# An attention and feed-forward kernel: four orders of loads on the SyncE queue

## The reference

```python
# x: (4, 1024, 512), ctx: (4, 2048, 512); 16 heads of width 32; all in float32
n = layernorm(x)
q, k, v = n @ W_q.T, ctx @ W_k.T, ctx @ W_v.T            # split into 16 heads
e = exp(clip(q @ k.T / sqrt(32), -50, 50))               # per head; mask keeps all rows
x = x + ((e / e.sum(-1)) @ v) @ W_o.T
n = layernorm(x)
# feed-forward: rows of n and columns of rhs scaled to whole numbers in -127..127
x = x + (round(n / s_n) @ round(rhs / s_r)) * s_n * s_r
```

## Time and profile before

| | |
|---|---|
| median of 3 runs | 1706.11 us (1705.11 to 1706.46) |
| the profiled execution's own time | 1705.6 us |
| its span | 1703.8 us |
| TensorE busy | 1671.9 us, 98% of the span |
| VectorE busy | 1489.7 us, 87% |
| ScalarE busy | 1314.5 us, 77% |
| GpSimd busy | 133.7 us, 8% |
| DMA queue of SyncE | 287.64 MB, 66.5% of 16 engines |
| on the chain that ended last | TensorE 82%, ScalarE 6%, DMA 5%, VectorE 4% |

### The profile page before, as it was taken

How to read it: one execution, slowest core, us unless ns; L and a number is a source line. 1 busy time by engine, 2 the same in 40 slices (tenths; PEclk the granted TensorE clock), 3 DMA queues, 4 the chain that set the end, 5 groups by cost and what they waited for, 6 DMA issues and landing times.

```text
span 1703.8 us, 29863 instructions
## 1 busy us (share of the span) xinstructions
PE 1671.9 (98%) x10418; PEld 1009.7 (59%) x10448; DVE 1489.7 (87%) x1705; ACT 1314.5 (77%) x1730; POOL 133.7 (8%) x75
## 2 busy tenths in 40 slices
PE   9999999999999999999999999999999999999998
PEld 8896655656565565656666566565656444444445
DVE  5657888888897989999898998989999889999997
ACT  5557788888887877877777787877878778788875
POOL 0000000000001111011110101111011000000001
PEclk9999999999999999999999999999999999999999
DMA  8687656566666566756657576566756799988971
GB/s 280 211 233 187 145 139 152 154 168 170 145 163 167 143 176 168 197 137 165 179 134 206 127 192 165 144 186 159 199 134 155 180 210 205 217 180 204 214 172 62
DMA packets 235059, 294.85 MB, mean 173 GB/s; under 512 B 28184, under 2 KB 142360, under 8 KB 234392
## 3 DMA queue, kind: packets, MB, share of 16 engines
q1 hardware_dynamic: 231688, 287.64, 66.5%
q10 hardware_dynamic: 3216, 5.24, 1.1%
HBM read 201.07 MB, written 91.48 MB: 172 GB/s over the span
## 4 chain that ended last, share of the span: by engine, by line
PE 82%; ACT 6%; DMA 5%; DVE 4%; issue 2%; SPq 1%; ACTq 0%; POOL 0%; POOLq 0%; DVEq 0%
PE wsum L999 25%; PE tile L962 24%; PE scores L984 21%; ACT probs L1247 5%; PE scores L1148 3%; PE scores L962 2%; DVE acc L1552 2%; PE tile L1148 1%; PE tile L1031 1%; DMA q_stack<-q_parts 1%; DMA row_lo<-o_parts 1%; DMA o_parts<-sums 1%; PE tile L1111 1%; DMA q_parts<-q_stack 1%; PE tile L1088 1%
## 5 line engine op out<-in xcount | busy, mean ns | idle before, releaser
L1247 ACT ACTIVATE probs<-scores 128x1024 f32<-128x1024 f32 x939 | 914.7, 1026 | 207.8 <-PE scores L984 169.3
L1552 DVE TENSOR_TENSOR acc<-acc,probs 128x2048 f32<-128x2048 f32 x439 | 1003.1, 2285 | 39.9 <-ACT probs L1247 25.3
L999 PE MATMUL wsum<-probs,v_sb 128*32 128x512 f32 x4096 | 492.4, 598 | 0.0
L984 PE MATMUL scores<-q_stack,k_stack 128*128 128x512 f32 x1536 | 444.5, 409 | 2.5 <-ACT probs L1247 1.7
L984 PEld LDWEIGHTS scores<-q_stack,k_stack 128*128 128x128 f32 x1536 | 264.9, 188 | 213.2 <-ACT probs L1247 121.3
L999 PEld LDWEIGHTS wsum<-probs,v_sb 128*32 128x32 f32 x4096 | 106.9, 109 | 243.9 <-issue 230.0
L1654 POOL TENSOR_TENSOR rstd<-var_eps,minus_half 128x1 f32<-128x1 f32 x48 | 105.9, 2207 | 1186.7 <-DVE var_eps L1446 1186.7
L1552 DVE TENSOR_TENSOR acc<-probs 128x2048 f32<-128x2048 f32 x32 | 73.4, 2293 | 56.7 <-PE tile L1031 51.2
L1148 PE MATMUL scores<-q_stack,k_stack 128*128 128x512 f32 x342 | 109.6, 421 | 8.6 <-ACT probs L1247 8.6
L962 PE MATMUL tile<-ctx_hi,wk_hi 128*128 128x256 f32 x412 | 116.4, 283 | 0.0
L962 PE MATMUL tile<-ctx_hi,wk_lo 128*128 128x256 f32 x412 | 116.0, 282 | 0.0
(11 more groups left out here) (255 smaller groups left out, 1988.4 us busy)
## 6 DMA issues: line engine op xcount, KB each, us to landing
k_stack<-k_parts SPq DMA_DIRECT2D x312, 256.0 KB, 7.8
q_stack<-q_parts SPq DMA_DIRECT2D x124, 256.0 KB, 7.2
v_sb<-v_parts SPq DMA_DIRECT2D x80, 256.0 KB, 7.5
v_parts<-v_stage SPq DMA_DIRECT2D x64, 256.0 KB, 5.0
raw<-ctxT SPq DMA_DIRECT2D x27, 512.0 KB, 5.6
k_parts<-stage_hi SPq DMA_DIRECT2D x96, 128.0 KB, 4.7
k_parts<-stage_lo SPq DMA_DIRECT2D x96, 128.0 KB, 2.5
x_in<-x SPq DMA_DIRECT2D x33, 256.0 KB, 4.2
```

Of the source, the lines that this page charges most:

```text
L984: last = nc.tensor.matmul(scores[:, h, :], k_stack[:, kt // 4, h, (kt % 4) * P:(kt % 4 + 1) * P], q_stack[:, qb, h, :], start=True, stop=True)
L999: last = nc.tensor.matmul(wsum[DH * h:DH * h + DH, :], v_sb[:, kt, DH * h:DH * h + DH], probs[:, n % RING, h, :], start=(kt == 0), stop=(k ...
L1247: nc.scalar.activation(probs[:, slot % RING, 2 * pair:2 * pair + 2, :], score_banks(seg, slot, pair), ACT.Exp, scale=1.0 / math.sqrt(DH)). ...
L1552: nc.vector.tensor_tensor(acc[:, :, :], other, probs[:, slot % RING, :, :], ALU.add).then_inc(sems["add_done"], 1)
```

## The change

Only the order of SyncE's instructions changes, with one semaphore name on TensorE.

```diff
-ROW_LOADS = {0: 0, 1: 5, 2: 5, 3: 5, 4: 1, 5: 1, 6: 7, ...}
+ROW_LOADS = {0: 0, 1: 5, 2: 4, 3: 4, 4: 1, 5: 1, 6: 7, ...}
# final_steps
                     if slot == 5 and c == 0:
-                        load_o_rows(sp, 0, slice(0, G), slice(P, QB), "rows_loaded5")
+                        load_o_rows(sp, 0, slice(0, G), slice(P, 2 * P), "rows_loaded5")
+                    if slot == 14 and c == 0:
+                        load_o_rows(sp, 0, slice(0, G), slice(2 * P, QB), "rows_loaded4")
...
-                        if step == 8:
+                        if step == (6 if i == 0 else 8):
                             load_q(sp, j_next, qb_next, (i + 1) % 2)
# iteration
-                    if seg.s == 0 and slot == 12:
+                    if seg.s == 1 and slot == 2:
+                        load_last()
+                    if seg.s == 1 and slot == 6:
                         load_weight("o", woT)
-                        load_last()
...
-                            if slot == KT + 4 * quarter + 5:
+                            if slot == KT + 4 * quarter + 5 + (quarter == 2):
                                 ct.wait_alone(sp, "scores_full", 2 * (KT + 4 * quarter + 4))
                                 load_k(sp, j + 1, quarter)
-                            if slot == KT + 4 * quarter + 6 + (quarter == 0) - (quarter == 2):
+                            if slot == KT + 4 * quarter + 6 + (quarter == 0):
                                 ct.wait_alone(sp, "step_summed", KT + 4 * quarter + 4)
                                 load_v(j + 1, quarter)
```

More of the change, by code:

```diff
@@ L161 @@
 D_BEFORE = order_of_the_bank()
-ROW_LOADS = {0: 0, 1: 5, 2: 5, 3: 5, 4: 1, 5: 1, 6: 7, 7: 7, 8: 2, 9: 2, 10: 6, 11: 6}
+ROW_LOADS = {0: 0, 1: 5, 2: 4, 3: 4, 4: 1, 5: 1, 6: 7, 7: 7, 8: 2, 9: 2, 10: 6, 11: 6}
 class Segment:
```

## The result

The kernel after takes 1754.49 us (median of 6 runs, 1751.27 to 1756.39) against 1706.28 us before (6 runs on the same chip): a ratio of 1.0278, with a 95% interval from 1.0265 to 1.029. It is slower, as forecast, but by 48 us where the forecast had 18, and it lies outside the range of 1706 to 1735. The profiled execution took 1751.27 us with a span of 1749.5, which is 45.7 us over the span of before.

The account below looks back on a forecast made before the run. The prediction took TensorE, busy 1671.9 of 1703.8 us, to bound the kernel. Its terms, -3.2 - 1.1 + 22.8 - 0.6 = +17.9 us on 1705.6, gave 1723.5, predicted as 1724, with a range from 1706 to 1735.

Parts of the forecast that it names:

- The opening, -3.2: Opening: weights issued behind the first stores remove TensorE's 1.70 us wait and 1.54 us of slow clock; -3.2 us.
- Changes of batch, -1.1: Two changes of batch: result stores ahead of keys shorten TensorE's waits for stage C's rows; -1.1 us, bounds -2.4 and +1.5.
- Nine borders, +22.8: Borders within batches: Q2's store behind keys delays ScalarE's cast and TensorE; 6 x 2.3 + 3 x 3.0 = +22.8 us.
- the second pair of heads: Nine borders: TensorE stands 0.3 us more at each, between the two pairs of heads.
- rival B: Nine borders: gaps also lower TensorE's clock, 1.54 us more at each, +13.9, giving 1738 us; chance 0.10.
- The last batch, -0.6: Last batch: the queries' wait goes, but `safe_row` lands later behind keys; net -0.6 us, bounds -1.5 and +2.5.
- 1 us of it comes out at the block's end: Last batch: VectorE's first sum starts some 3 us later, of which 1 us was counted as cost.
- The -1.5 for the queries: Last batch: TensorE's 1.48 us wait for the second block's queries goes once they move ahead of the keys.
- Rivals A: Nine borders: stores pass the keys or ScalarE's delay is hidden, so they cost nothing; 1701 us, chance 0.14.
- C: Nine borders: Q2's store lands 7 us after the first key issue, +4.2 us in all; 1705 us, chance 0.09.
- the two halves of the rule: DMA queues: descriptors are taken in ring order, holding a store behind keys; completion isn't first in, first out, letting it pass.

Follow-up runs that it names:

- experiments 1: The kernel after with the third quarter of keys and values back in slot 29 at every part; 1702.94 us, ratio 0.9976.
- experiment 8: The kernel before with: opening's edit alone, 1702.21 us; last batch's edits alone, 1703.71 us; opening's edit and quarter moved at ends of batches 0 and 1, 1701.91 us.
- experiments 2: The kernel before with only the third quarter of keys and values moved to slot 30; 1753.30 us, ratio 1.0273.
- experiments 3: The kernel after with the third quarter of keys and values moved only at the ends of batches 0 and 1; 1701.74 us, ratio 0.9974.
- experiment 4: The kernel after with the third quarter of keys and values issued, within a batch, behind the stores of Q2 and Q3; 1741.06 us, ratio 1.02.
- 5: The kernel after with Q2's and Q3's four stores issued, within a batch, from ScalarE's queue behind its exponentials of slot 31; 1722.93 us, ratio 1.0112.
- Experiment 7: The kernel after with small products ahead of slot 2's scores in batch 0's three borders: 24 products, 1750.98 us; 14 products, 1750.81 us.
- experiment 9: The kernel after with: quarter back within batches, behind `safe_row` in batch 2, 1704.29 us; `safe_row` on GpSimd's queue, 1752.99 us; that with keys mostly back, 1703.42 us.
- experiment 6: The kernel after with only the third quarter's values in slot 30, 1700.98 us; with only its keys in slot 30, 1731.14 us.
- the last of 8: The kernel before with the opening's loads moved and the quarter moved only at the ends of batches 0 and 1; 1701.91 us, ratio 0.9976.
- the first two of 8: The kernel before with the opening's edit alone, 1702.21 us; and with only the last batch's edits, 1703.71 us.
- the last run of experiment 9: Opening as in after, keys late only at ends of batches 0 and 1, values late except batch 2's end, `safe_row` on GpSimd's queue, queries ahead; 1703.42 us.

## Why the prediction was wrong in size

- **The opening, -3.2.** Measured -3.35 in the profiled execution. As a step it stood, but its 1.54 us of clock belonged to that one execution of before: two unchanged openings ran 1.70 and 2.45 us ahead of it, with PEclk 1.00. That the number came out so near is partly luck.
- **Changes of batch, -1.1.** Measured -2.7, a little past the low bound of -2.4. Both waits of the earlier trace rows are gone: the rows land 3.4 us behind TensorE's last mark of the batch (534.7 against 531.35) where they took 5.3 (522.8 against 517.43); I had forecast a gain of 1.2 us for 2.0 measured. Part of this belongs to the one execution of before as well. With the quarter left in its place, three other executions (experiments 1 and 8) stepped by -0.08, -0.43 and -1.46 us at the first change and by +0.15, -0.38 and +0.06 at the second; with it moved, they stepped by -0.6 to -2.4 and by -0.1 to -1.0 in experiments 2 to 5 and 7 to 9. And since the values alone bring as much (experiment 6), the keys ahead of the result were not the whole of what made its rows late, as my sum had it.
- **Nine borders, +22.8. This is the step that failed, by its size.** The mechanism is shown (experiments 1, 2, 4 and 6): loads issued ahead of the store, buffer, cast, exponential, scores, in the order forecast. The term measured 47.5 us, for three reasons. Q2's store landed 10.1 us after the first key issue, where I took 9.0, between the two cases of its own kind, 9.7 and 9.8, and a key load with little around it; even my high bound was 9.8. That makes the idle time 30.1 us instead of the 20.1 forecast (2.0 and 2.7 a border; the rest of the 22.8 was 0.3 a border for the second pair of heads). Then I put the lower clock aside as rival B, with a chance of 0.10, because two gaps of 1.86 and 1.48 us had been followed by full clock; but the gaps I was forecasting were longer, 2.3 and 3.0 us, and the only evidence I had against B came from shorter ones. B was not another way for it to go; it was part of the same sum. But shorter gaps are not safe either: in experiment 6 the clock fell behind 1.79 us and not behind 2.13. The Trainium skill tells in "TensorE: Matmul & The Clock Gate", "HAM oscillation — how this bites in real kernels", of a loop whose wait for a DMA, some 3 to 5 us, comes back in every round, so that every round starts with the array at the low clock. The nine gaps here, 2.44 to 4.24 us, did the same. Last, I counted 0.3 us for the second pair of heads, where ScalarE's delay costs TensorE about 0.9 us behind the gap. Experiment 7 splits what lies behind the gaps of batch 0 in halves: 1.0 us a border of clock, 0.9 of this. For the other six the split was not measured directly (experiment 6 puts the clock at 1.2 us a border); the two make 17.4 us over the nine, where the sum had 2.7.
- **The last batch, -0.6.** Measured +4.3, outside -1.5 to +2.5. `safe_row` took 4.5 us as forecast (4.7), and VectorE was 2.35 us late for my 3. What I guessed, that 1 us of it comes out at the block's end, can't be read from this one execution. Experiments 4 and 7 (with 24 products) have the same instructions in the last batch, `safe_row` in 4.5 and 4.4 us, and VectorE 2.4 and 2.2 us late, and their last batch steps by +1.45 and +1.25, within my bounds. VectorE's first sum in experiment 4, 34.8 us after its counterpart of before where TensorE's lag is 32.4:

```profile
1370.78 2.29 DVE L1560 TENSOR_TENSOR acc<-probs 128x2048 f32<-128x2048 f32 x1 [1.17 <-POOLq L1688]
```

The first block costs 1.7, 1.7 and 1.5 us in the three. The second costs 2.7 in the kernel after and nothing in the other two, so the late flag doesn't force it. The -1.5 for the queries was wrong: the 1.5 us came back as waits for VectorE (experiments 1 and 8). The rows in two pieces cost nothing by themselves: with them, the queries ahead and an early flag the last batch steps by +0.1 (experiment 8).

- **Rivals A and C** (hidden, 1701 and 1705) are excluded by the borders' rows: no landing came under 9.2 us. (By the prediction's own sum C costs 1.0 us, not 0.8, at a border of batch 0, which changes nothing.) B, 1738, named the clock and was still short, since it left the landing and the second pair as they were. Of the two halves of the rule that the prediction weighed (the Trainium skill, "DMA: Bandwidth & Descriptors", "Queues, rings and completion order"), the nine landings agree with the order of the ring, and no store here passed the loads ahead of it in its own queue.

Open: why `safe_row` took 3.7, 2.9 and 3.5 us in experiments 3 and 1 and the last of 8, where before took 1.80 and the first two of 8 took 1.95 and 1.69, with the same issues ahead of it in all six. Open too is what makes the last batch's second block cost 2.7 us in some executions and nothing in others, and whether it was a queue or the order of issue over all queues that held the stores.

## What to carry to other kernels

When a load is moved ahead of a store in a queue, price the wait of whoever writes that store's buffer next, by landings of the same kind (stores behind such loads: 9.7 and 9.8 us here, for 10.1 measured), and don't shade them towards faster ones of another kind. An idle gap on TensorE in a kernel at full clock can have three prices, not one: the gap, the slower clock behind it, and the engine that fed it running late; where a rival can only add to the forecast's own mechanism, it belongs in the sum. Where the engine beside TensorE has little room, a gain may not be kept: in the last batch's first two blocks before, VectorE is busy for 79.5 of 86 us and TensorE for 81.3, and a wait removed came back under another name. And a step of 1 or 2 us read from one execution against another can be that execution's own.

## What the runs showed of the hardware

- Behind the nine gaps of the kernel after, 2.44 to 4.24 us, the granted clock fell each time, at 322, 421 and 625 to 0.50 (1.2 GHz) for some 3, 6 and 6 us. In the run with the keys only it fell behind gaps of 1.79 to 3.50 us at six borders and stayed at 1.00 behind 0.98, 1.22 and 2.13 us; in the kernel before it stayed behind 1.48 and 1.86 us and fell behind 1.70. Small products in the gap kept it at 1.00.
- A store of 128 KB behind 1.25 MB in the same queue landed 9.2 to 10.9 us after the first load's issue. Issued from ScalarE's queue 0.2 us behind the first load, it landed 5.8 us after that load's issue (4.2 to 6.3 over nine borders), always behind the load issued before it and ahead of the one issued after it.
- A load of 16 numbers from an otherwise idle queue took 6.4 us, with 2.25 MB issued on SyncE's queue in the 5 us before it, and 3.3 us in the last run of experiment 9, where the last issue before it stood 3.8 us ahead.
